# Two layers of cross-attention and mixture of experts: DMAs place the second attention's keys in a cleared array

## The reference

```python
x = x + L0_xattn(layernorm(x), ctx)   # 8 heads of 64, keys of 154 rows, softmax
x = x + L0_ffn(layernorm(x))          # 16 experts of 64, top 4 in top 2 of 4 groups, + a shared expert
x = x + L1_xattn(layernorm(x), ctx)   # 16 heads of 8
x = x + L1_ffn(layernorm(x))          # 8 experts of 256, top 2, + a shared expert
```

```python
q = (x @ Wq).reshape(B, SQ, 16, 8).transpose(0, 2, 1, 3)
k = (ctx @ Wk).reshape(B, SKV, 16, 8).transpose(0, 2, 1, 3)
scores = jnp.einsum('bhqd,bhkd->bhqk', q, k) / sqrt(8)
weights = softmax(scores)
```

## Time and profile before

| what | value |
|---|---|
| median of 3 runs | 232.13 us (232.04 to 232.33) |
| span of the profiled execution | 229.8 us |
| median less the span (what lies around it) | 2.3 us |
| PE busy | 223.2 us (97%) |
| DVE busy | 163.5 us (71%) |
| ACT busy | 155.3 us (68%) |
| POOL busy | 126.4 us (55%) |

### The profile page before, as it was taken

How to read it: one execution, slowest core, us unless ns; L and a number is a source line. 1 busy time by engine, 2 the same in 40 slices (tenths; PEclk the granted TensorE clock), 3 DMA queues, 4 the chain that set the end, 5 groups by cost and what they waited for, 6 DMA issues and landing times.

```text
span 229.8 us, 4648 instructions
## 1 busy us (share of the span) xinstructions
PE 223.2 (97%) x1389; PEld 166.4 (72%) x1389; DVE 163.5 (71%) x480; ACT 155.3 (68%) x378; POOL 126.4 (55%) x127
## 2 busy tenths in 40 slices
PE   7999999999999999999999999999999999999994
PEld 3576765974989898889535563588878887888873
DVE  3689984788667953699948983564857776776874
ACT  2589999986678446662689788876365686645561
POOL 2766742898057927856592107209499400996540
PEclk9999999999999999999999999999999999999999
DMA  6890000000038924800600000037000003600002
GB/s 208 198 303 8 0 3 0 0 3 1 3 93 230 365 105 165 203 0 4 219 3 0 7 0 6 0 82 287 3 0 0 1 3 105 265 0 4 1 0 91
DMA packets 10174, 17.07 MB, mean 74 GB/s; under 512 B 3715, under 2 KB 5540, under 8 KB 9766
## 3 DMA queue, kind: packets, MB, share of 16 engines
q1 hardware_dynamic: 9926, 16.45, 23.1%
q10 hardware_dynamic: 224, 0.32, 0.4%
HBM read 16.08 MB, written 0.62 MB: 73 GB/s over the span
## 4 chain that ended last, share of the span: by engine, by line
PE 83%; ACT 6%; DVE 3%; DMA 2%; SPq 2%; POOL 2%; issue 1%; DVEq 0%; POOLq 0%
PE psum L1170 12%; PE psum L1173 11%; PE psum L1171 11%; PE psum L1326 7%; ACT prob L748 5%; PE psum L1384 5%; PE psum L1333 4%; PE psum L1335 3%; PE psum L1334 3%; PE psum L1435 3%; PE psum L1278 3%; PE psum L1288 3%; PE psum L1404 2%; PE psum L1256 2%; PE psum L1245 2%; DMA ctxT<-in_ctxT 2%
## 5 line engine op out<-in xcount | busy, mean ns | idle before, releaser
L702 POOL TENSOR_TENSOR act_s<-act_s,spread 128x512 f32<-128x512 f32 x35 | 44.4, 1292 | 19.8 <-DMA spread<-cw 13.6
L1170 PE MATMUL psum<-xT_hi,w_hi 128*128 128x512 f32 x108 | 43.9, 406 | 0.0
L1173 PE MATMUL psum<-xT_lo,w_hi 128*128 128x512 f32 x108 | 42.2, 391 | 0.0
L1171 PE MATMUL psum<-xT_hi,w_lo 128*128 128x512 f32 x108 | 42.2, 391 | 0.0
L797 ACT CAST q<-psum 128x512 fp32r<-128x512 f32 x35 | 20.4, 586 | 20.3 <-PE psum L1335 13.7
L1006 DVE TENSOR_TENSOR q<-psum,q 128x512 fp32r<-128x512 f32 x35 | 23.8, 687 | 13.3 <-ACT q L797 13.0
L787 ACT ACTIVATE act_s<-psum 128x512 f32<-128x512 f32 x39 | 23.0, 597 | 12.3 <-PE psum L1173 7.9
L1143 DVE TENSOR_REDUCE neg_max<-psum 128x2 f32<-128x308 f32 x64 | 26.2, 471 | 4.9 <-PE psum L1384 4.7
L702 POOL TENSOR_TENSOR hid<-hid,spread 128x512 f32<-128x512 f32 x13 | 16.6, 1297 | 18.9 <-DMA spread<-cw 14.6
L652 POOL TENSOR_TENSOR rstd<-vareps,minus_half 128x4 f32<-128x4 f32 x8 | 8.1, 1014 | 33.9 <-DVE vareps L907 33.9
L646 POOL TENSOR_TENSOR w_lo<-w_src,w_hi 128x768 fp32r<-128x768 f32 x12 | 21.7, 1830 | 8.9 <-ACT w_hi L717 8.9
(11 more groups left out here) (171 smaller groups left out, 468.2 us busy)
## 6 DMA issues: line engine op xcount, KB each, us to landing
spread<-cw SPq DMA_DIRECT2D x16, 256.0 KB, 4.4
spread<-cw SPq DMA_DIRECT2D x6, 512.0 KB, 5.5
w_src<-in_w SPq DMA_DIRECT2D x2, 1152.0 KB, 5.3
w_src<-in_w SPq DMA_DIRECT2D x1, 2304.0 KB, 12.4
spread<-cw SPq DMA_DIRECT2D x8, 128.0 KB, 2.9
w<-in_w SPq DMA_DIRECT2D x1, 576.0 KB, 6.9
out<-X SPq DMA_DIRECT2D x4, 128.0 KB, 1.8
wv<-in_wv SPq DMA_DIRECT2D x2, 192.0 KB, 4.8
```

The lines of the kernel that those rows point to most:

```text
L702: pool.tensor_tensor(g, g, spread[:, slot, :], ALU.mult).then_inc(weighed, 1)
L1170: pe.matmul(dst, w_hi, xT_hi[:, b, :], start=True, stop=False)
L1171: pe.matmul(dst, w_lo, xT_hi[:, b, :], start=False, stop=False)
L1173: return pe.matmul(dst, w_hi, xT_lo[:, b, :], start=False, stop=True)
```

## The change

Placing the keys moves from ACT to DMAs. DVE clears the whole array k1 at its start, right behind the clearing of act_s. `k_stack` gets room for all four groups, and DVE's k1 step no longer waits for the placing of an earlier group. A new step "place_k1" of SP issues, for each group g, four DMAs that copy the 32 rows of each head from the stack into the cleared array, and each group has a semaphore of its own. ACT's sixteen multiplications are gone. Beside that the orders of all five engines and the banks are written anew:

- DVE: before it began "lnA sel lnA xT vf1 q q vf xT score", now "lnA lnA xT q q vf vf1 score xT score"; sel stands among the scores.
- ACT: before "kT split lnB kT xT kT kT lnB q", now "kT split lnB kT kT xT lnB q kT xT q".
- POOL: the two bo and the four place_k1s stand elsewhere (before, two place_k1s ran in front of the first weigh and two among later splits; now all four run before the first weigh).
- SP: place_k1 of group 0 stands in front of the last spread of the first batch, group 1 behind the second store, group 2 behind the third spread of batch 1, group 3 behind its last.
- PE: the first q products follow the same seven steps as before (vf one place earlier); one h1 now stands before the last three pT of batch 1; the FFN and attention steps of the later stages are interleaved otherwise.

```diff
-    steps += [("place_k1", g, j) for g in groups for j in range(4)]
+    steps += [("place_k1", g) for g in groups]
...
 PROGRAM = {
     "PE":
-        "kT.0 kT.1 kT.0 kT.2 xT.3 vf.1 vf1.4 q.2 q.3 q.4 xT.2 q.3 scores.4.0 scores.3.1 scores.2.5 scores.6.7 " +
...
+        "kT.0 kT.1 kT.2 vf.3 xT.4 kT.5 vf1.6 q.7 q.0 q.1 xT.2 q.4 scores.7.0 scores.5.1 scores.3.6 q.4 " +
...
     "ACT":
-        "kT split lnB kT xT kT kT lnB q xT q split " + 16 * "score " +
...
+        "kT split lnB kT kT xT lnB q kT xT q score score score score split score score score score score score " +
...
     "DVE":
-        "lnA sel lnA xT vf1 q q vf xT " + 9 * "score " +
...
+        "lnA lnA xT q q vf vf1 score xT score score q score score score score norm score q score q vf score norm " +
...
     "SP":
-        "store spread spread spread spread spread fetch store spread spread spread spread spread place_max " +
-        "fetch place_max place_max place_max store spread spread spread spread spread store spread spread " +
-        "spread spread spread out out out out ",
+        "store spread spread spread spread place_k1 spread fetch store place_k1 spread spread spread place_k1 " +
+        "spread spread place_k1 place_max place_max place_max fetch place_max store spread spread spread spread " +
+        "spread store spread spread spread spread spread out out out out ",
...
-                    k_stack = sb("k_stack", [P, 2, B * CP], F32R, r3)
+                    k_stack = sb("k_stack", [P, G1, B * CP], F32R, r3)
...
+                elif kind == "place_k1":
+
+                    g = step[1]
+                    sp.wait_ge(k1_cleared, 1)
+                    wait_moved(sp, ("k1", g))
+                    k = k_stack[:, g, :].bitcast(F32).rearrange("p (b c) -> p b c", b=B)
+                    for j in range(4):
+                        rows = slice(PAD * j, PAD * j + PAD)
+                        sp.dma_start(k1[rows, :, g, j, :].bitcast(F32), k[rows, :, 0:CTX]).then_inc(k1_placed[g], 16)
...
-                    act.mul(k1[:, :, g, j, :], k[:, :, 0:CTX], head_rows[:, j:j + 1]).then_inc(k1_placed, 1)
...
             dve.memset(act_s[:, 0, :], 0.0).then_inc(idle_ready, 1)
+            dve.memset(k1[:, :, :, :, :].bitcast(F32).rearrange("p b g j c -> p (b g j c)"), 0.0).then_inc(k1_cleared, 1)
...
-                    if g >= 2:
-
-                        dve.wait_ge(k1_placed, 4 * (g - 1))
-                        dve.wait_ge(k1s_placed, g - 1)
...
-                    pe.wait_ge(k1_placed, 4 * (g + 1))
+                    pe.wait_ge(k1_placed[g], 16 * 4)
```

More of the change, by code:

```diff
@@ L206 @@
-    "Pool":
-        "lnA split lnA bo bo split " + 7 * "norm " + "lnA norm place_k1s split split split lnA place_k1s " +
-        8 * "weigh " + "split split lnA " + 8 * "weigh " +
-        "split split lnA split place_k1s place_k1s split split split lnA split split weigh weigh weigh weigh " +
-        "weigh lnA " + 27 * "weigh ",
[24 rows of a table added]
+    "ACT":
+        "kT split lnB kT kT xT lnB q kT xT q score score score score split score score score score score score " +
+        "score score score score score score pT pT k1 score score pT score score pT split score score pv pv " +
+        "score pv score pv score score score score score split score score score pT lnB k1 k1 xT pT pT k1 split " +
+        "split pT gate h1 pv pv pv pv cwT h1 lnB h1 h1 h1 xT gate h1 h1 h1 h1 cwT h1 split h1 h1 h1 lnB h1 xT " +
+        "split qd q1copy q1copy h1 q1copy q1copy h1 split h1 h1 split split mT exp expR exp exp exp expR lnB xT " +
+        "exp exp mT qd exp exp q1copy q1copy q1copy expR q1copy expR exp exp exp split exp od exp mT exp exp exp " +
+        "od exp exp exp expR exp onT expR mT exp exp exp exp expR lnB expR xT exp exp exp exp exp exp od exp " +
+        "route exp h1 cwT h1 od hsplit hsplit h1 split h1 split onT h1 split h1 h1 hsplit hsplit h1 h1 h1 hsplit " +
+        "hsplit h1 h1 hsplit hsplit h1 hsplit lnB h1 hsplit h1 hsplit xT h1 h1 hsplit hsplit hsplit hsplit route " +
+        "hsplit h1 h1 hsplit h1 cwT h1 hsplit h1 hsplit h1 h1 h1 hsplit hsplit hsplit hsplit h1 ycopy ycopy h1 " +
+        "h1 hsplit hsplit h1 h1 h1 hsplit hsplit h1 hsplit hsplit h1 hsplit hsplit h1 hsplit h1 hsplit h1 hsplit " +
+        "hsplit ycopy ycopy ",
@@ new lines @@
+    "DVE":
+        "lnA lnA xT q q vf vf1 score xT score score q score score score score norm score q score q vf score norm " +
+        "score score pT pT score score norm vs score score score pT pT norm q score pT pT score k1 score pT pT " +
+        "score sel score score norm score score norm score score score score score norm pT wo pT wo score lnA " +
[8 rows of a table added]
+        "hsplit xT h3 hsplit gate hsplit route h3 hsplit hsplit h3 hsplit h3 route h3 hsplit hsplit h3 hsplit h3 " +
+        "h3 hsplit hsplit h3 h3 hsplit hsplit h3 h3 h3 hsplit h3 hsplit hsplit h3 hsplit hsplit h3 hsplit h3 h3 " +
+        "hsplit h3 hsplit h3 hsplit hsplit h3 h3 hsplit hsplit h3 res res res last_res res last_res ",
@@ new lines @@
+    "Pool":
+        "lnA split lnA split norm norm norm norm norm place_k1s bo norm split norm lnA norm place_k1s place_k1s " +
+        "place_k1s bo split split lnA split weigh weigh weigh weigh weigh weigh weigh weigh lnA weigh weigh " +
+        "weigh weigh split weigh weigh weigh split split weigh split split lnA split lnA split weigh weigh weigh " +
+        "weigh split weigh weigh weigh weigh weigh weigh weigh lnA weigh weigh weigh split weigh weigh weigh " +
+        "weigh weigh weigh weigh weigh weigh weigh weigh weigh weigh weigh weigh weigh weigh weigh ",
@@ L421, in build @@
         k1_rounded = sem("k1_rounded")
-        k1_placed = sem("k1_placed")
+        k1_cleared = sem("k1_cleared")
+        k1_placed = [sem(f"k1_placed{g}") for g in range(G1)]
         sel_built = sem("sel_built")
@@ L810, in _ @@
                     act.copy(rounded[:, g % 2, 0:B * CP], bank(step)[:, 0:B * CP]).then_inc(k1_rounded, 1)
-                elif kind == "place_k1":
-                    g, j = step[1:]
-                    wait_moved(act, ("k1", g))
-                    act.wait_ge(loaded["const"], 16 * N_CONST)
-                    k = k_stack[:, g % 2, :].bitcast(F32).rearrange("p (b c) -> p b c", b=B)
-                    act.mul(k1[:, :, g, j, :], k[:, :, 0:CTX], head_rows[:, j:j + 1]).then_inc(k1_placed, 1)
                 elif kind == "qd":
@@ L857, in _ @@
                         wait_filled(act, ("oT", 0, k))
-                    act.wait_ge(k1_placed, 4 * G1)
+                    for g in range(G1):
+                        act.wait_ge(k1_placed[g], 16 * 4)
                     act.wait_ge(k1s_placed, G1)
```

26 lines of the change are left out of this document (2 added, 24 removed), and 57 rows, old and new, of the table PROGRAM.

## The result

The changed kernel takes 234.9 us (median of 4 executions, 233.34 to 236.27) where the kernel before takes 232.1 on the same chip: ratio 1.0125, 95% interval 1.0075 to 1.0174. It is slower by 2.8 us, the prediction said slower by 0.7. The profiled execution took 234.22 us with a span of 232.4, against 229.8 before. The prediction's three terms, and one that it did not have, turn out as follows. Each measured price is the difference of two kernels' ratios to the kernel before, times 232 us; the error behind it is an estimate, made from the two runs' 95% intervals.

A forecast was written before the change was run, and what follows sets the result against it. The prediction took TensorE's nearly full stream to bound the kernel, so the start counts. Its terms, +1.3 (clear), +0.2 (SP's queue) and -0.8 (orders), sum to +0.7 us: 232.8 us, range 231.0 to 234.4.

The forecast's parts named there:

- The prediction's three terms: Clear at the start +1.3 us, placing DMAs on SP's queue +0.2, new orders and banks -0.8.
- the term for new orders and banks: Attention stages: a quarter of 3.3 us of ScalarE waits and TensorE idle is won, -0.8 us (0 to -3.3).
- The term for SP's queue: Placing DMAs among the spreads make spreads slightly late for POOL: +0.2 us (0 to 1.0).
- What bounds the kernel: TensorE's nearly full stream; ScalarE time saved in full stages buys nothing, delay before the first real product is not absorbed.
- Removal of ScalarE's multiplications: Sixteen ScalarE placing multiplications leave, ten of them between 57 and 80 us: 0.0 us taken from the removal itself.
- The clear, +1.3: Start: VectorE's 4.67 us memset delays bn_stats, so the first q matmul starts near 11.4 instead of 10.12: +1.3 us.
- The rival of the cheap memset: Start: the memset runs at half the time per element and slack swallows it; 231.5 us, chance 0.13.
- The step "TensorE still without gaps in 57 to 110": Sign to look for in the changed kernel's timeline: TensorE shows no gap from 57 to 110 us.
- the sign named for a wrong prediction: Prediction wrong if the first q starts by 10.5 us or the second attention's waits fall by more than half.
- Start plus spreads late: Start costs in full and displaced spreads make POOL late: +2.3 us, 234.4 us, chance 0.07.
- The clock rival: Start: idleness before the first q drops TensorE's clock to half for ten products, about 2.3 us; 235.1 us, chance 0.03.

The follow-up runs named there:

- e16: Changed kernel, its POOL order kept, but the first of the two weighings ahead of the last batch's norm waits for VectorE's vareps: 232.78 us, ratio 1.0062.
- e17: e8 with the first of the two weighings ahead of the last batch's norm waiting for VectorE's vareps: 229.95 us, ratio 0.9925.
- e12: Kernel before, orders and banks kept, placing DMAs replacing ScalarE's multiplications (groups 2 and 3 behind the first five spreads), clear on POOL: 233.2 us, ratio 1.0069.
- e14: Changed kernel with POOL's norm of the last batch moved ahead of the two weighings before it: 232.56 us, ratio 1.0036.
- e18: e1 with POOL's norm of the last batch moved ahead of the two weighings before it: 230.97 us, ratio 0.9965.
- e4: Kernel before with only VectorE's clear of k1 added at the start: 233.41 us against 232.06, ratio 1.0079.
- e1: Changed kernel with k1 cleared by POOL ahead of its batch 1 norm before the first routed layer, not by VectorE at the start: 231.8 us, ratio 1.0002.
- e7: Changed kernel, clear at the start kept, with all sixteen placing DMAs ahead of batch 0's store: 234.95 us, ratio 1.0155.
- e10: Changed kernel with neg_mean and vareps computed by POOL instead of VectorE: 237.08 us, ratio 1.0241.
- e8: Changed kernel with the clear on POOL ahead of its gates split and all placing DMAs ahead of the first store: 232.16 us, ratio 1.0002.
- e5: Changed kernel with two more 512-column multiplications on TensorE before the first transposes: 235.16 us, ratio 1.0158.
- e6: Changed kernel with VectorE clearing batch 0's half of k1 at the start and POOL the other half late: 232.01 us, ratio 1.0023.
- e15: e8 with POOL's norm of the last batch moved ahead of the two weighings before it: 229.92 us, ratio 0.9922.
- e11: e8 with neg_mean and vareps computed by POOL instead of VectorE: 234.04 us, ratio 1.0104.
- e3: e1 with all sixteen placing DMAs right behind the w13_1 weight fetch: 233.79 us, ratio 1.0073.

## Why the prediction was off, step by step

The step that failed is the term for new orders and banks: it counted only what the new orders could win (0 to -3.3 us) and put what they could cost at nothing, without a reason. The runs show in its place a meeting of VectorE and POOL at 170 us, which one wait removes (e16, e17), at 0.9 to 2.1 us by the pair of runs that one takes. The term for SP's queue was mis-sized as well, 1.0 us for 0.2.

- **What bounds the kernel** held. TensorE's stream is what counts, ScalarE's relief in the full stages bought nothing: 6 us of it left the window from 57 to 110, and e12 shows the same without the new orders.
- **Removal of ScalarE's multiplications, 0**: right.
- **The clear, +1.3**: the mechanism was right, the size somewhat low. By ratio from the small memset it was to take 4.67 us; its row says 4.17, the engine was held for 5.07. The first q came at 11.66 (predicted 11.4), the first exponential at 16.5 (predicted 16.4). The ratio of e14 to e18 gives 1.65 us, e4 gives 1.8 (1.35 by its medians), e1 against the changed kernel 2.85. The rule of the Trainium skill (VectorE: DVE Perf Modes, "Zero memsets can be issued as uint32"), one cycle per element, an estimate of 5.13 us at the page's clock, was nearer than the ratio between rows; the measured 5.07 us agrees with it. The rival of the cheap memset is refuted.
- **SP's queue, +0.2 (0 to 1.0)**: mis-sized, it is 1.0 us, the upper end. The working looked closely at batch 0's last spread and gave groups 1 to 3 half a sentence ("do the same to batch 1's spreads"). For batch 0 it was right: the last spread landed at 76.88 and 77.90 (predicted 77.3 and 77.9), and POOL did not wait for it. Group 1 stands ahead of all of batch 1's spreads, and batch 1 is where POOL has just been waiting for its norm and weighs each chunk as it lands. The step "TensorE still without gaps in 57 to 110" failed with it. The w13_1 fetch went out at 74.31, as predicted.
- **Orders, -0.8 (0 to -3.3)**: mis-sized, they gain 1.8 us. The waits of the score1 weight loads, 7.3 us in the earlier trace rows and 0.7 more for issue, are down to 3.7, so the sign named for a wrong prediction came true. The term assumed that waits for VectorE's neg_max (5.1 us) have no cure while VectorE keeps its 64 reductions. They have: in the changed kernel they are 0.2 us. How much of the 1.8 us this is, no run parts. The reductions are as many, only other matmuls stand between a score1 and the bank that it needs:

```profile
L1385 PEld LDWEIGHTS psum<-k,q x64: 186/188/203, 95.8 to 135.1; 128*128 128x128 f32 x64
...
  issue: 2.4, 5
  ACT probT L848: 0.5, 2
...
  DVE neg_max L1144: 0.2, 1
```

- **What was missing, +2.1 (0.9 by e1 and e18)**: the working read none of the orders for what they bring together: that POOL's new order puts seven weighings ahead of the norm at 170 us, where it was idle in the kernel before. With the meeting gone from the changed kernel (e16), 232.78 us was measured where 232.8 was predicted, by three sizes that cancel: that is luck, no credit to the working.
- **The rivals.** Start plus spreads late came nearest (234.4 for 234.9), and its mechanism is there, as 2.65 of the loss; it had 7 in 100. The clock rival named the start. In e7 and e10, which clear at the start too, a stretch at the lower level did follow the stand there (1.93 and 2.28 us), and in e8 it followed the stand at 171; in e5 a stand of 1.94 us at 174 had none behind it. In the changed kernel's profile the lower level comes only after the last products, but two of its four executions have a mean clock below 0.995 and are the two longest. So part of its median may be the clock's; how much, four executions can't tell.

A small stand is left unexplained: in the changed kernel TensorE loses about 0.3 us near 200 us behind a spread that comes late after everything else is late; no run was made for it.

## What to carry to other kernels

Before a clear, a copy or any new work is put at the start of an idle engine, find out how much of that idleness is slack to the first product: here 2.5 us were free (e6) and 5 cost 1.65 or more. When an order is changed, read every engine pair for what now runs side by side, not only for who waits for whom; a tiny VectorE operation between two engines' long ones can be held for as long as the neighbour's work lasts, and one wait that keeps the neighbour still for 0.17 us saved some 1.5 to 1.8 us. When DMAs are added to an in-order queue, price them at every burst that they are put into, and by what is in flight, not at the first burst alone.

The version to keep is e15 (or e17): the changed kernel with the clear on POOL ahead of the gates split, the placing DMAs ahead of the first store, and the last norm ahead of two weighings, at 229.9 us, 0.8% faster than the kernel before.

## What the runs showed of the hardware

- A VectorE tensor_scalar of 128x4 took 0.17 us with POOL idle and 0.47, 1.33 and 2.97 us beside POOL's back-to-back 128x512 products of two tiles. Wherever it was held, its end fell on the end of a POOL instruction; at 2.97 us it waited out the one that was running and two more. It was also held beside POOL's single splits: neg_mean for 1.08 us in e1 at 8.76, vareps for 1.81 us in e12 at 88.07. VectorE's 128x512 operations with one operand in PSUM kept their 0.67 to 0.69 us beside the same POOL work.
- A memset of 4,928 fp32 elements a partition held VectorE for 5.07 us, while its row shows 4.17 us and 0.97 us of "issue" ahead of it, the same in two kernels. Half of it held VectorE for 2.49 us, with a row of 2.11 (e6). The row of a long memset is not its price.
- The 38.5 KB SBUF-to-SBUF DMAs landed 1.9 us after issue with free DMA engines (e8), 3.5 us among spreads and 8.6 us behind a 2.3 MB fetch (medians), at about 0.6 us of queue time each (median 0.60 in e3 and the changed kernel).
- After stands of 1.9 to 2.3 us TensorE's granted clock was at 1.2 GHz for a stretch (e7, e8, e10), and in e11 after two of 0.27 and 0.78 us within 3 us; after e5's 1.94 us, e3's 1.56, the same pair of 0.27 and 0.78 us in e10, and the 0.6 us stands of the changed kernel's and e1's profiles, it was not. So the lower level followed some stands and not others, which is one source of the spread between executions (e8: 230.3 to 233.7 us; e17, with no stand above 0.3 us, 229.93 to 230.15). It is not the only one: four of e8's executions with a mean clock of 1.0 lie between 232.1 and 232.6 us.
